# Twelve expert chunks instead of nine inside the four-head attention of a graph network, the expert biases on GpSimd, and twelve buffers for the stored parts

## The chip, the core and the metric

The kernel runs on one core of a Trainium2 chip. The metric is the device time of one execution in microseconds (us). Before the change it was 8173.12 us in the median of three runs (8167.27, 8173.12 and 8198.01).

## The reference

Four layers of a network on a graph of 6250 nodes with 256 features and 106250 edges, each added to its input: an edge adapter, six experts with a router, a graph attention of two layers with one head, and four experts whose router is a graph attention with four heads. The change lies in the last of them, of which this is the part that matters (131072 edges of its own and a loop for each of the 6250 rows):

```python
h = (x_flat @ W_gat).reshape(M, HEADS, NUM_EXPERTS)
a_src = (h * att_src).sum(-1)
a_dst = (h * att_dst).sum(-1)
e = leaky_relu(a_src[src] + a_dst[dst], negative_slope=0.2)
e_max = segment_max(e, dst)
ee = jnp.exp(e - e_max[dst])
alpha = ee / (segment_sum(ee, dst)[dst] + 1e-16)
agg = segment_sum(h[src] * alpha[:, :, None], dst).reshape(M, HEADS * NUM_EXPERTS) + b_gat
scores = layernorm(agg, ln_gamma, ln_beta).reshape(M, HEADS, NUM_EXPERTS).mean(1)
topk_s, topk_i = top_k(scores, 2)
w = softmax(topk_s, axis=-1)
for ei in range(NUM_EXPERTS):                       # 4 experts
    g = jnp.where(topk_i == ei, w, 0.0).sum(-1)
    hh = gelu(x @ W1[ei] + b1[ei])                  # 256 -> 512
    out = out + g[..., None] * (hh @ W2[ei] + b2[ei])   # 512 -> 256
```

The experts' values hh @ W2 don't depend on the router, only the gates g do. That is why the kernel can compute them before the scores are known.

## The kernel before, in words

The 6250 nodes lie in 49 blocks of 128 rows (NB), four blocks are a chunk (CB), so there are twelve full chunks and one of a single block (chunk 12, NCH). XT holds the normalized input, transposed, for all blocks. One *unit* is one chunk with one expert. A unit has eight products, each a sum over TensorE matmuls into one PSUM bank, pE: four of the first layer (128 of the 512 hidden values for 512 nodes, line 876) and four of the last layer (one block of 128 nodes by 256 values, line 881).

The four-head attention (function attention with H = 4) walks over 304 groups (NGS) of 512 edges that are sorted by their target block. Each engine has its own instruction list, written out group by group by the helper pipeline: for each iteration it calls a list of parts, each for a group that lies some groups ahead or behind. What ties the engines together are semaphores, and each engine executes its list strictly in order. In one iteration `it`

- GpSimd gathers the rows of G for a group with four indirect DMAs (line 782), up to eight groups ahead (RING);
- TensorE does lookup (pL, line 840), sums (pU, line 859), then one expert product (dense_product), then spread (pT, line 816, and pW, line 820) for the next group and turn_scores (pA, line 802) for the one behind it;
- ScalarE does dense_drain (it copies pE out, a first-layer product with its bias to hid, line 983, a last-layer product to ystage, line 987), near (ST, line 919), copies (aT, line 901), rescale (alpha, line 936), weights (p, line 967, and S, line 970), dense_gelu (the gelu over the hidden values of a unit when its fourth first-layer product has been drained, line 997), distances (Nm, line 928) and node_bits (lines 911 and 912, which turn_scores needs);
- VectorE does several_heads: the reduction mt<-pW (line 1072), pf = G x p (line 1080), and a chain of small instructions up to acc (line 1156);
- SP stores each drained last-layer block from ystage to expert_parts in DRAM (line 767).

Before the change the expert products begin in group 8 (FIRST), one in each group, and cover PRE = 9 chunks, 36 units, 288 products. First-layer products of a unit alternate with last-layer products of the unit before it (dense_step). A product may start when the one before it has been drained from pE (s_xd).

The last block (last_experts) computes the four chunks that are left, 16 units, of which the last four are of one block: hidden (pH, line 2077) and last (pO, line 2088) on TensorE, gelu and a drain to one of three buffers yr on ScalarE (lines 2107 and 2114). VectorE first computes the scores and the gates (lines 2134 to 2183), with a square root (line 2120) and an exp by ScalarE in between. Then it merges the units in the order of the list todo: the fresh ones of this block, with the 36 stored ones (yl, read back by SP through three buffers of 512 KB, line 2040) spread evenly between them. A unit gets its bias B2 (with_bias, line 2200) and is then added to X with its gate, one instruction a block (line 2210). When the last expert of a chunk has been added, SP stores the chunk's rows to the output. ScalarE's list has the first fresh unit's drain behind the square root.

Of the kernel before, what the change touches and what calls it, by code (L numbers as in the profile page):

```python
# [14 lines left out]
ALU = mybir.AluOpType  # L15
ACT = mybir.ActivationFunctionType
# [7 lines left out]
P = 128  # L24
N = 6250
D = 256
KT = D // P
NB = -(-N // P)
TAIL = N - (NB - 1) * P
CB = 4  # L30
# [19 lines left out]
RING = 8  # L50
# [6 lines left out]
HID = 512  # L57
# [4 lines left out]
PADS = P  # L62
PRE = 9
UNITS = PRE * 4
FIRST = 8
# [591 lines left out]


def attention(self, gi, H, F, table, acc, m, adst, dense=None):

# [6 lines left out]
    v = nc.vector  # L667
    one = H == 1
    NG, K = NGS[gi], KS[gi]
# [10 lines left out]
    with ctx:  # L680
# [63 lines left out]
        def _(sp):  # L744
# [12 lines left out]
            for g in range(NG):  # L757
                part, n = g // PART + 1, g - FIRST
                if g % PART == RING and 2 <= part < NG // PART:
                    sp.wait_ge(s_U, (part - 1) * PART)  # L760
                    load(part)
                if not one and 0 <= n < 8 * UNITS:
                    hidden, u, i = dense_step(n)
                    if not hidden:
                        c, x = u // NX1, u % NX1
                        sp.wait_ge(s_xd, n + 1)
                        sp.dma_start(y_dram[c * P:(c + 1) * P, (x * CB + i) * D:(x * CB + i + 1) * D], ystage[:, i, :])\
                            .then_inc(s_ys[i], 16)
# [18 lines left out]
        def _(pe):  # L787
# [74 lines left out]

            def dense_product(g, j, turn):

                n = g - FIRST
                if not 0 <= n < 8 * UNITS:
                    return
                hidden, u, i = dense_step(n)
# [16 lines left out]
            if one:  # L885
                pipeline(pe, NG, [(2, turn_scores), (1, spread), (-2, turn_weights), (-3, sums)], RING)
            else:
                pipeline(pe, NG, [(-1, lookup), (-4, sums), (0, dense_product), (1, spread), (2, turn_scores)], RING)

        @block.scalar  # L890
        def _(act):
# [79 lines left out]

            def dense_drain(g, j, turn):

                n = g - FIRST
                if not 0 <= n < 8 * UNITS:
                    return
                hidden, u, i = dense_step(n)
# [11 lines left out]
            def dense_gelu(g, j, turn):  # L989

                n = g - FIRST
                if not 0 <= n < 8 * UNITS:
                    return
                hidden, u, i = dense_step(n)
                if hidden and i == HID // P - 1:
                    act.wait_ge(s_xd, n + 1)
                    a.activation(hid[u % 2], hid[u % 2], ACT.Gelu).then_inc(s_gelu, 1)

            if one:
                pipeline(act, NG, [(0, score), (0, rescale), (2, copies), (3, node_bits), (-2, copy_weights), (0, weights)], RING)  # L1000
            else:
                pipeline(act, NG, [(0, dense_drain), (1, near), (2, copies), (0, rescale), (-1, weights), (0, dense_gelu),
                                   (1, distances), (3, node_bits)], RING)

# [985 lines left out]
def last_experts(self, XT, acc, dense):  # L1990
# [6 lines left out]
    left = [(c, e) for c in range(PRE, NCH + 1) for e in range(E)]  # L1997
    SLOTS, RY = 3, 3
    ctx, sb, ps, sem = self.scope()
    with ctx:  # L2000
# [6 lines left out]
               sb("yr2", [P, CB, D])[:, :, :]]  # L2007
        yl = sb("yl", [P, RY, CB, D])
        bg, ga, be = (sb(x, [P, NH]) for x in ("bg", "ga", "be"))
# [18 lines left out]
        def blocks(c):  # L2028
            return min(CB, NB - c * CB)

        todo, ready = [], [(c, e) for c in range(PRE) for e in range(E)]
        for n, unit in enumerate(left):
# [4 lines left out]
        def _(sp):  # L2037
            def load(n):
                c, e = ready[n]
                sp.dma_start(yl[:, n % RY, :, :].rearrange("p i d -> p (i d)"),  # L2040
                             y_dram[c * P:(c + 1) * P, e * CB * D:(e + 1) * CB * D]).then_inc(s_yl[n % RY], 16)
# [8 lines left out]
            for n, (c, e) in enumerate(todo):  # L2050
# [12 lines left out]
                if c == NCH:  # L2063
                    sp.dma_start(self.out[(NB - 1) * P:N, :], self.X[0:TAIL, NB - 1, :]).then_inc(s_out, 16)
                    outs += 1
            sp.wait_ge(s_out, 16 * outs)

        @block.tensor
# [60 lines left out]
        def _(dve):  # L2129
# [54 lines left out]

            def part(unit):
                cc, e = unit
                n = blocks(cc)
                if cc < PRE:
                    return yl[:, ready.index(unit) % RY, 0:n, :]
                return yr[left.index(unit) % SLOTS][:, 0:n, :]  # L2190

            def with_bias(n):
                cc, e = todo[n]
                if cc < PRE:
                    k_ = ready.index(todo[n])
                    dve.wait_ge(s_yl[k_ % RY], 16 * (k_ // RY + 1))
                else:
                    dve.wait_ge(s_od, left.index(todo[n]) + 1)
                t = part(todo[n])
                v.tensor_tensor(t, t, B2[:, e, :].unsqueeze(1).to_broadcast([P, blocks(cc), D]), ALU.add).then_inc(s_t, 1)  # L2200

            def add(n):
# [9 lines left out]

            with_bias(0)
            for n in range(len(todo)):
                nxt = n + 1 < len(todo)
                if nxt:
                    with_bias(n + 1)
                add(n)
# [72 lines left out]
```

## Time and profile before

| | before |
|---|---|
| median of three runs | 8173.12 us |
| profiled execution | 8179.65 us |
| span of its trace | 8177.9 us |
| four-head attention, first to last reduction | 6373.8 to 7944.6 us |
| last block, first product to end of the span | 7960.1 to 8177.9 us |
| last addition of the last block ends | 8173.2 us |
| busy over the whole span: TensorE, VectorE, ScalarE, GpSimd | 54%, 66%, 44%, 72% |

A profile is of one execution. In it PE is TensorE's matmul, PEld its weight load, DVE is VectorE, ACT ScalarE, POOL GpSimd and SP the engine that issues most transfers. Times are us from the start of the span. All other blocks of the kernel, up to 6370 us, are the same in both versions.

### The profile page before, as it was taken

The page shows a single profiled execution, that of the slowest core. Times are in us where ns is not written, and L with a number is a line of the kernel's source. Part 1 is how long each engine was busy: PE and PEld are TensorE (multiplying, and loading weights), DVE is VectorE, ACT ScalarE, POOL GpSimd, SP SyncE. Part 2 cuts the span into 40 slices and gives each one's busy share as a digit, 9 for nine tenths or more (in the row PEclk, how much of TensorE's full clock was granted, in tenths as well). Part 3 has the DMA queues.
Part 4 walks back from the last instruction along what each step waited for, and adds up shares of the span by engine and source line. Part 5 has one row for each costly group of instructions (what it writes and reads, how often), then busy time and mean ns, then how long its engine had stood idle before and what let it go on. Part 6 is the DMA issues. An engine that isn't in the chain of part 4 may idle for free. (4 is left out here: it accounts for less than half of the span.)

```text
span 8177.9 us, 116177 instructions
## 1 busy us (share of the span) xinstructions
PE 4396.1 (54%) x22490; PEld 2786.9 (34%) x22610; DVE 5392.1 (66%) x18777; ACT 3584.6 (44%) x11436; POOL 5852.7 (72%) x6709
## 2 busy tenths in 40 slices
PE   0000008915269992466666656666612677777768
PEld 0000007912135551344444434444411344444435
DVE  9999308913112221577777767777741899999987
ACT  0000003401012220277777547777721688888872
POOL 2777777777777777777777777777777777777750
PEclk9999999956589996699999979999966799999989
DMA  5111111200010000134434323444310211111113
GB/s 160 26 25 26 24 22 42 47 2 3 2 29 1 1 1 1 51 107 108 108 108 108 84 74 107 108 108 108 107 29 5 41 28 27 28 27 28 28 32 117
DMA packets 476255, 426.34 MB, mean 52 GB/s; under 512 B 269726, under 2 KB 409876, under 8 KB 475668
## 3 DMA queue, kind: packets, MB, share of 16 engines
q0 software_dynamic: 214016, 282.62, 15.0%
q1 hardware_dynamic: 224020, 120.13, 5.4%
q10 hardware_dynamic: 37632, 17.48, 0.9%
q14 instruction: 428, 3.51, 0.1%
q8 instruction: 159, 2.61, 0.1%
HBM read 341.50 MB, written 78.72 MB: 51 GB/s over the span
## 5 line engine op out<-in xcount | busy, mean ns | idle before, releaser
L438 POOL DMA_INDIRECT pay_sorted<-pay,pos x1856 | 1857.5, 1001 | 667.6 <-issue 291.9
L782 POOL DMA_INDIRECT G<-tab_gat,pay x1856 | 1788.9, 964 | 591.4 <-issue 559.0
L782 POOL DMA_INDIRECT G<-tab_rt,pay x1216 | 1154.4, 949 | 427.5 <-issue 298.0
L275 POOL DMA_INDIRECT attr_sorted<-rows,pos x832 | 841.4, 1011 | 389.2 <-issue 253.1
L856 PE MATMUL pU<-G,PM 128*128 128x257 f32 x3712 | 994.0, 391 | 2.5 <-DVE acc L1169 2.4
L802 PE MATMUL pA<-identb,G 128*20 128x128 bf16 (+1 forms) x3072 | 388.5, 226 | 943.8 <-DMA G<-tab_gat,pay 810.6
L901 ACT ACTIVATE aT<-pA 20x256 bf16<-20x256 bf16 (+1 forms) x1232 | 519.2, 421 | 527.3 <-PE pA L802 517.8
L1072 DVE TENSOR_REDUCE mt<-pW 128x4 f32<-128x2048 f32 x304 | 694.5, 2285 | 14.3 <-PE pW L820 12.9
L856 PEld LDWEIGHTS pU<-G,PM 128*128 128x128 f32 x3712 | 652.6, 196 | 59.0 <-ACT PM L953 3.0
L802 PEld LDWEIGHTS pA<-identb,G 128*20 128x20 bf16 (+1 forms) x3072 | 163.9, 92 | 1451.7 <-DMA G<-tab_gat,pay 1196.7
L323 ACT ACTIVATE rows<-lo 128x16 f32<-128x16 f32 x52 | 11.6, 229 | 1138.4 <-DMA attr_sorted<-rows,pos 1078.8
L947 ACT ACTIVATE e<-pW,adst 128x256 f32<-128x256 f32 x928 | 431.2, 465 | 172.9 <-DVE mt L1045 127.0
L1045 DVE TENSOR_REDUCE mt<-pW 128x1 f32<-128x256 f32 x928 | 390.7, 421 | 124.8 <-PE pW L812 116.9
L1673 DVE TENSOR_TENSOR t<-pO,BL 128x1024 f32<-128x1024 f32 (+1 forms) x78 | 90.7, 1163 | 573.7 <-PE pO L1620 573.6
L1657 ACT ACTIVATE H<-pH,B 128x512 f32<-128x512 f32 (+1 forms) x312 | 206.5, 662 | 593.0 <-PE pH L1609 592.1
L1169 DVE SCALAR_TENSOR_TENSOR acc<-acc,alpha,pU 128x257 f32 x928 | 442.6, 477 | 25.9 <-issue 17.4
L962 ACT ACTIVATE PT<-e,bias 128x256 f32<-128x256 f32 x928 | 456.5, 492 | 0.7 <-DVE e L1161 0.7
L1161 DVE SCALAR_TENSOR_TENSOR e<-e 128x256 f32<-128x256 f32 x928 | 397.7, 429 | 36.9 <-ACT e L947 2.9
L928 ACT ACTIVATE Nm<-iota,pay 128x128 bf16<-128x128 f32 x1216 | 383.2, 385 | 0.0
L828 PE MATMUL pP<-ident,PT 128*128 128x128 f32 x1856 | 364.3, 279 | 0.0
L336 PE MATMUL turned<-ident,gsum 128*1 128x128 f32 x24 | 5.6, 411 | 632.7 <-DVE gsum L406 632.7
L953 ACT ACTIVATE PM<-pP 128x256 f32<-128x256 f32 x928 | 332.0, 358 | 8.5 <-PE pP L828 7.8
(327 smaller groups left out, 11639.2 us busy)
## 6 DMA issues: line engine op xcount, KB each, us to landing
pay_sorted<-pay,pos POOLq DMA_INDIRECT x1856, 2.1
G<-tab_gat,pay POOLq DMA_INDIRECT x1856
G<-tab_rt,pay POOLq DMA_INDIRECT x1216, 2.4
expert_parts<-pos SPq DMA_DIRECT2D x144, 128.0 KB, 1.7
yl<-expert_parts SPq DMA_DIRECT2D x36, 512.0 KB, 3.8
attr_sorted<-zattr SPq DMA_DIRECT2D x1, 16896.0 KB, 53.4
rows<-attr_sorted ACTq DMA_DIRECT2D x256, 66.0 KB
attr_sorted<-rows,pos POOLq DMA_INDIRECT x832, 2.2
```

The lines of the kernel that those rows point to most:

```text
L275: pool.indirect_dma_start(out=self.attr_sorted, out_offset=bass.IndirectOffsetOnAxis(ap=pos0[:, t:t + 1], axis=0), in_=rows[:, j, k, :], i ...
L438: pool.indirect_dma_start(out=out, out_offset=bass.IndirectOffsetOnAxis(ap=self.pos[g][:, lo + n:lo + n + 1], axis=0), in_=self.pay[g][:, ...
L782: pool.indirect_dma_start(out=G[:, j, k, 0:R], out_offset=None, in_=table, in_offset=bass.IndirectOffsetOnAxis(ap=pay[:, g % (2 * PART), k ...
L802: ins = nc.tensor.transpose(pA[j % len(pA)][:, k * P:(k + 1) * P], parts[:, k, 0:ROWS], self.identb[:, :])
L856: ins = nc.tensor.matmul(u[:, 0:F], PM[:, j % 2, k * P:(k + 1) * P], G[:, j, k, 0:F], start=(k == 0), stop=(k == K - 1))
L901: a.activation(aT[0:ROWS, j % 2, :], pA[j % len(pA)][:, 0:K * P], ACT.Copy).then_inc(s_aT, 1)
L947: a.activation(e[:, j % 2, :], pW[j % 2][:, 0:K * P], ACT.Identity, bias=ad).then_inc(s_y, 1)
L962: a.activation(PT[:, s, :], e[:, s, :], ACT.Exp, bias=bias[:, j % 4:j % 4 + 1]).then_inc(s_PT, 1)
L1045: v.tensor_reduce(mt, pW[s][:, 0:K * P], AX.X, ALU.max).then_inc(s_max, 1)
L1072: v.tensor_reduce(mt, pW[:, :, :], AX.X, ALU.max).then_inc(s_max, 1)
L1161: v.scalar_tensor_tensor(e[:, j % 2, :], e[:, j % 2, :], SLOPE, e[:, j % 2, :], ALU.mult, ALU.max).then_inc(s_e, 1)
L1169: v.scalar_tensor_tensor(ac, ac, alpha[:, j, 0:1], pU[j % 2][:, 0:F], ALU.mult, ALU.add).then_inc(s_acc, 1)
```

## The change

PRE goes from 9 to 12, so that all twelve full chunks are computed inside the attention: 48 units, 384 products. The function quanta says which products a group takes: two in every third group from group 8 on, one in the others, 384 in 288 groups. The second product of a group is the last of TensorE's iteration, and its drain stands behind weights on ScalarE. In the last block only chunk 12, one block of 128 rows, is left to compute, four units. The stored parts, now 48, come back through twelve buffers, which lie in the columns of XT that no one reads any more. The biases are added by GpSimd, in the order of todo, and VectorE keeps the gated additions.

```diff
-PRE = 9
+PRE = 12
...
+def quanta(g):
+
+
+    at = g - FIRST
+    if at < 0:
+        return []
+    n = at + (at + 2) // 3
+    return [x for x in (n, n + 1)[:2 if at % 3 == 0 else 1] if x < 8 * UNITS]
...
             def dense_product(g, j, turn):
-
-                n = g - FIRST
-                if not 0 <= n < 8 * UNITS:
-                    return
+                for n in quanta(g)[0:1]:
+                    product(n)
+
+            def second_product(g, j, turn):
+                for n in quanta(g)[1:2]:
+                    product(n)
...
-                pipeline(pe, NG, [(-1, lookup), (-4, sums), (0, dense_product), (1, spread), (2, turn_scores)], RING)
+                pipeline(pe, NG, [(-1, lookup), (-4, sums), (0, dense_product), (1, spread), (2, turn_scores), (0, second_product)], RING)
...
-                pipeline(act, NG, [(0, dense_drain), (1, near), (2, copies), (0, rescale), (-1, weights), (0, dense_gelu),
-                                   (1, distances), (3, node_bits)], RING)
+                pipeline(act, NG, [(0, dense_drain), (1, near), (2, copies), (0, rescale), (-1, weights), (0, second_drain),
+                                   (0, dense_gelu), (1, distances), (3, node_bits)], RING)
...
-    SLOTS, RY = 3, 3
+    SLOTS, RY = 3, 12
...
-        yl = sb("yl", [P, RY, CB, D])
+        of_k = RY // KT
+
+        def yl(n):
+            return XT[:, n % RY // of_k, n % of_k * CB * D:(n % of_k + 1) * CB * D]
+
...
+        @block.gpsimd
+        def _(pool):
+            pool.wait_ge(s_w, 64)
+            for n, (c, e) in enumerate(todo):
+                if c < PRE:
+                    k_ = ready.index((c, e))
+                    pool.wait_ge(s_yl[k_ % RY], 16 * (k_ // RY + 1))
+                else:
+                    pool.wait_ge(s_od, left.index((c, e)) + 1)
+                t = part((c, e))
+                pool.tensor_tensor(t, t, B2[:, e, :].unsqueeze(1).to_broadcast([P, blocks(c), D]), ALU.add).then_inc(s_t, 1)
+
...
-            with_bias(0)
             for n in range(len(todo)):
-                nxt = n + 1 < len(todo)
-                if nxt:
-                    with_bias(n + 1)
                 add(n)
```

How the instructions lie on the engines is shown at three places; in the rows a number x4 is a count of equal instructions, and the line numbers of the changed kernel are some 10 to 40 higher. First TensorE, one iteration in the middle of the attention, before:

```order
L840 MATMUL pLU<-tabs,pay 128x24 x4
L859 MATMUL pLU<-pfs,pay 128x60 x4
L876 MATMUL pE<-XT,W 128x512 x2
L816 MATMUL pT<-aT,sel 128x512
L820 MATMUL pW<-aT,sel 128x512 x4
L802 MATMUL pA<-identb,G 28x128 x4
```

The same place in the changed kernel, an iteration of a group with two products:

```order
L850 MATMUL pLU<-tabs,pay 128x24 x4
L869 MATMUL pLU<-pfs,pay 128x60 x4
L891 MATMUL pE<-XT,W 128x512 x2
L826 MATMUL pT<-aT,sel 128x512
L830 MATMUL pW<-aT,sel 128x512 x4
L812 MATMUL pA<-identb,G 28x128 x4
L896 MATMUL pE<-W,pay 128x256 x4
```

The second product, a last-layer one, stands between turn pA and the next iteration's lookup. Next ScalarE, from the drain of a unit's fourth first-layer product over its gelu to the next drain, before:

```order
L983 ACTIVATE pay<-pE,B 128x512
L919 ACTIVATE pay<-pT 128x512
L901 ACTIVATE aT<-pA 28x512
L936 ACTIVATE alpha<-dm 128x4
L967 ACTIVATE p<-d 128x16
L970 ACTIVATE pay<-Nm 128x512
L997 ACT_TABLE_LOAD
L997 ACTIVATE pay<-pay 128x2048
L928 ACTIVATE Nm<-iota,pay 128x128 x4
L911 ACTIVATE G<-pay 128x4x8
L912 ACTIVATE G<-pay 128x4x8
L987 ACTIVATE pos<-pE 128x256
```

And the changed kernel, from the second drain of the group before it to the gelu:

```order
L1007 ACTIVATE pos<-pE 128x256
L943 ACTIVATE Nm<-iota,pay 128x128 x4
L926 ACTIVATE G<-pay 128x4x8
L927 ACTIVATE G<-pay 128x4x8
L1003 ACTIVATE pay<-pE,B 128x512
L934 ACTIVATE pay<-pT 128x512
L916 ACTIVATE aT<-pA 28x512
L951 ACTIVATE alpha<-dm 128x4
L982 ACTIVATE p<-d 128x16
L985 ACTIVATE pay<-Nm 128x512
L1015 ACT_TABLE_LOAD
L1015 ACTIVATE pay<-pay 128x2048
```

A second drain now stands ahead of the distances, the bits and all that follows them up to the gelu. Last VectorE in the last block, from the gates on, before:

```order
L2183 TENSOR_TENSOR pos<-pos 128x196
L2200 TENSOR_TENSOR pos<-pos,B_21 128x1024
L2200 TENSOR_TENSOR yl<-yl,B_21 128x1024
L2210 SCALAR_TENSOR_TENSOR X<-pos,X 128x256 x4
L2200 TENSOR_TENSOR yl<-yl,B_21 128x1024
L2210 SCALAR_TENSOR_TENSOR X<-yl,pos,X 128x256 x4
L2200 TENSOR_TENSOR pay<-pay,B_21 128x1024
```

VectorE at the same place in the changed kernel:

```order
L2223 TENSOR_TENSOR pos<-pay,m_21 128x196
L2224 TENSOR_TENSOR pos<-pos 128x196
L2234 SCALAR_TENSOR_TENSOR X<-pos,X 128x256
L2234 SCALAR_TENSOR_TENSOR X<-XT,pos,X 128x256 x48
L2234 SCALAR_TENSOR_TENSOR X<-pay,pos,X 128x256
```

And GpSimd there, which had no instruction in this block before:

```order
L690 UNCONDITIONAL_BRANCH
L2097 UNCONDITIONAL_BRANCH
L2107 TENSOR_TENSOR pos<-pos,B_21 128x256
L2107 TENSOR_TENSOR XT<-XT,B_21 128x1024 x12
L2107 TENSOR_TENSOR pay<-pay,B_21 128x256
```

The biases have moved from VectorE to GpSimd, and the first of them is that of the first fresh unit; twelve stored parts follow each fresh one.

## Rows read from the trace of the kernel before

**Rows 1.** Busy us and counts of each engine by stretch, clock, DMA share.

```profile
6900.00:7100.00 200.00, 146.24 (x874) 82.07 (x889) 187.90 (x812) 162.55 (x473) 146.72 (x155) 0.97 0.17 28
8140.00:8160.00 20.00, 1.61 (x8) 1.08 (x6) 18.44 (x36) 0.69 (x2) 0.00 (x0) 0.62 0.62 196
```

**Rows 2.** One line's instructions (ns min/median/max, first and last start), and one wait.

```profile
L1072 DVE TENSOR_REDUCE mt<-pW x304: 2283/2284/2292, 6373.8 to 7944.6; 128x4 f32<-128x2048 f32 x152
...
L997 ACT ACTIVATE pay<-pay x36: 1909/1910/1914, 6434.8 to 7884.5; 128x2048 f32<-128x2048 f32 x36
...
DVE pf L1080 <- ACT p L967: 12.2, 28, 2.0
```

**Rows 3.** Timeline (start, us, engine, line) of one undisturbed period of the attention.

```profile
7031.96 2.28 DVE L1072 TENSOR_REDUCE mt<-pW 128x4 f32<-128x2048 f32 x1
...
7032.54 1.97 PE L881 MATMUL pE<-W,pay 128*128 128x256 f32 x8
...
7035.52 0.40 PE L802 MATMUL pA<-identb,G 128*28 128x128 bf16 x4
...
7036.64 0.61 ACT L970 ACTIVATE pay<-Nm 128x512 bf16<-128x512 bf16 x1
...
7036.99 2.28 DVE L1072 TENSOR_REDUCE mt<-pW 128x4 f32<-128x2048 f32 x1
...
7037.22 0.25 PE L840 MATMUL pLU<-tabs,pay 128*128 128x24 bf16 x4 [1.31 <-DVE acc L1156]
```

**Rows 4.** Timeline from a gelu's table load to the late pf and the next turn.

```profile
7010.91 1.28 ACT L997 ACT_TABLE_LOAD   x1
...
7015.66 0.38 PE L802 MATMUL pA<-identb,G 128*28 128x128 bf16 x4 [1.40 <-ACT G L912]
...
7018.39 0.24 DVE L1080 TENSOR_TENSOR pf<-G,p 128x80 f32<-128x80 f32 x1 [0.44 <-ACT p L967]
...
7020.42 0.38 PE L802 MATMUL pA<-identb,G 128*28 128x128 bf16 x4 [1.36 <-ACT G L912]
```

**Rows 5.** Chain that ended last (start, us, what): first, middle and last piece.

```profile
7960.11 15.91 PE pH L2077 x32
...
8129.38 1.03 ACT yr L2114
...
8172.37 0.79 DVE X L2210 x2
```

**Rows 6.** Timeline of the last block: square root, gates, two units' additions.

```profile
7978.23 0.24 ACT L2120 ACTIVATE mu<-var 128x49 f32<-128x49 f32 x1 [7.05 <-DVE var L2157]
...
7993.87 0.36 DVE L2183 TENSOR_TENSOR pos<-pos 128x196 f32<-128x196 f32 x1
...
8131.58 1.67 DVE L2210 SCALAR_TENSOR_TENSOR X<-yl,pos,X 128x256 f32<-128x256 f32 x4
...
8134.30 1.67 DVE L2210 SCALAR_TENSOR_TENSOR X<-yr,pos,X 128x256 f32<-128x256 f32 x4
```

**Rows 7.** Timeline of a period with a slow product.

```profile
7000.26 2.29 DVE L1072 TENSOR_REDUCE mt<-pW 128x4 f32<-128x2048 f32 x1
...
7000.84 3.16 PE L881 MATMUL pE<-W,pay 128*128 128x256 f32 x8
...
7005.61 2.29 DVE L1072 TENSOR_REDUCE mt<-pW 128x4 f32<-128x2048 f32 x1 [0.23 <-PE pW L820]
```

**Rows 8.** GpSimd's groups by line (count, busy us, mean ns, idle before).

```profile
L254 POOL MEMSET zattr<- 128x256 f32 x1 | 0.3, 311 | 0.7 <-POOLq L126 0.7
...
L190 POOL TENSOR_SCALAR_AFFINE_SELECT ident<-ident 128x128 f32<-128x128 f32 x1 | 0.3, 292 | 0.2 <-POOL identb L187 0.2
```

**Rows 9.** Timeline of GpSimd's scatters beside VectorE in the six-expert layer.

```profile
3005.26 0.97 POOL L438 DMA_INDIRECT pay_sorted<-pay,pos  x1 [0.30 <-issue]
...
3006.19 1.67 DVE L1680 SCALAR_TENSOR_TENSOR X<-t,g,X 128x256 f32 x4
...
3006.73 1.19 POOL L438 DMA_INDIRECT pay_sorted<-pay,pos  x1 [0.28 <-POOL idle L443]
```

More of the change, by code:

```diff
@@ L757, in _ @@
             for g in range(NG):
-                part, n = g // PART + 1, g - FIRST
+                part = g // PART + 1
                 if g % PART == RING and 2 <= part < NG // PART:
@@ L761, in _ @@
                     load(part)
-                if not one and 0 <= n < 8 * UNITS:
+                for n in () if one else quanta(g):
                     hidden, u, i = dense_step(n)
@@ L863, in dense_product, with product @@
             def dense_product(g, j, turn):
-                n = g - FIRST
-                if not 0 <= n < 8 * UNITS:
-                    return
+                for n in quanta(g)[0:1]:
[3 more added lines that the diff above has]
+                    product(n)
+            def product(n):
                 hidden, u, i = dense_step(n)
@@ L972, in dense_drain, with second_drain, drain @@
             def dense_drain(g, j, turn):
-                n = g - FIRST
-                if not 0 <= n < 8 * UNITS:
-                    return
+                for n in quanta(g)[0:1]:
+                    drain(n)
+            def second_drain(g, j, turn):
+                for n in quanta(g)[1:2]:
+                    drain(n)
+            def drain(n):
                 hidden, u, i = dense_step(n)
@@ L989, in dense_gelu @@
             def dense_gelu(g, j, turn):
[L991 to L997, printed above, removed]
+                for n in quanta(g):
+                    hidden, u, i = dense_step(n)
+                    if hidden and i == HID // P - 1:
+                        act.wait_ge(s_xd, n + 1)
+                        a.activation(hid[u % 2], hid[u % 2], ACT.Gelu).then_inc(s_gelu, 1)
             if one:
@@ L2029, in blocks, with part @@
             return min(CB, NB - c * CB)
+        def part(unit):
+            cc, e = unit
+            n = blocks(cc)
+            if cc < PRE:
+                return yl(ready.index(unit)).rearrange("p (i d) -> p i d", d=D)[:, 0:n, :]
+            return yr[left.index(unit) % SLOTS][:, 0:n, :]
         todo, ready = [], [(c, e) for c in range(PRE) for e in range(E)]
@@ L2039, in load @@
                 c, e = ready[n]
-                sp.dma_start(yl[:, n % RY, :, :].rearrange("p i d -> p (i d)"),
+                sp.dma_start(yl(n),
                              y_dram[c * P:(c + 1) * P, e * CB * D:(e + 1) * CB * D]).then_inc(s_yl[n % RY], 16)
@@ L2183, in _ @@
             c(v.tensor_tensor(g[:, :, :], a[:, :, :], b[:, :, :], ALU.add))
[L2185 to L2200, printed above, removed]
             def add(n):
```

## The prediction, made before the changed kernel was run

> **What bounds the kernel now.** I first asked where the kernel can change at all. All edits lie in the last two blocks, the four-head attention and the block of the last experts, so I read those two alone: first busy time by stretch, then single periods, then the chain that ended last. In the middle of the attention VectorE is busy for 187.9 of 200 us, ScalarE for 162.6, TensorE for 146 and GpSimd for 147 [rows 1]. One period of the loop is one group, and the longest instruction in it, VectorE's reduction mt<-pW, marks its start. 304 reductions start between 6373.8 and 7944.6 [rows 2], a mean of 5.18 us; an undisturbed period lasts 5.03 (7031.96 to 7036.99), with a product in it (pE<-W) [rows 3]: one product hides. VectorE sets the pace, and about 303 x 0.15 = 45 us of the block are lost elsewhere.
>
> The reader should look at ScalarE after a gelu. Table load and gelu take 1.28 and 1.91 us [rows 2, 4]; the bits that turn pA needs stand behind them, so TensorE waits 1.40 us for ScalarE, and behind that the weights p come late: VectorE's pf waits 0.44 us for them [rows 4]. Over the block pf waits 12.2 us for p, 28 times for 36 gelus [rows 2].
>
> In the last block the chain runs along TensorE's products from 7960.11 to the last drain at 8129.38, then along VectorE to 8173.16 [rows 5]: TensorE bounds it, with a tail on VectorE of 2.72 us a unit (8131.58 to 8134.30), of which 1.67 us are the four additions and the other 1.05 the bias, L2200 [rows 6].
>
> **Part 1, products in the attention.** 96 more products (12 units of 8) are fitted into the same 288 groups: every third group has a second product, which TensorE runs behind turn pA, as its last work of the period. Laid on the undisturbed period [rows 3]: turn pA ends 3.96 us after the reduction's start, and the next lookup starts at 5.26, so 1.30 us are free; the product takes 1.97. It runs 0.67 us into the next period, where the lookup has room. But its drain is queued on ScalarE behind S (which ends at 5.29) and waits for the product: 3.96 + 1.97 + 0.38 = 6.3, with the semaphores 1.33 us into the next period. The next product shares pE and waits for this drain: it starts at 1.35 and not at 0.58, so everything that ScalarE does behind its own drain is 0.78 us later in that period. Without a gelu the third group recovers this, and I cost that at nothing: the cover is the slack of ScalarE and TensorE against VectorE's 5.03; without it each second product costs what a slow product costs below.
>
> With a gelu it isn't recovered. A unit's last first-layer drain always falls in the group right behind a double one (it is product 8u+2, and the groups take products 4k and 4k+1, then 4k+2, then 4k+3 in turn), so each gelu starts 0.78 us later than now, and pf waits 0.44 + 0.78 = 1.22 us. There are 48 gelus then: 58.6 us against 12.2, +46. The delayed period is itself a double one. Its pf comes at about 2.2 + 1.22 = 3.4 us, the bits some 2.0 us behind it as now (7018.39 to 7020.42) [rows 4], and its first drain, 0.7, behind these: 6.2. Only then can its second product start; it ends 1.9 us into the next period (which begins at 6.25), its drain at 2.3, and that period's own product and spread (1.97 and 1.2, partly overlapped) at about 5.4: 0.37 us over 5.03. 48 x 0.37 = +18. Together **+64 us**.
>
> Bounds: if the later start is absorbed, only 12 more gelus at 12.2/36 = 0.34 us remain, +4. At the other end, where a product took 3.16 us and not 1.97 the period grew to 5.35 (7000.26 to 7005.61) [rows 7]; if each of the 96 costs these 0.32 us besides, +95. GpSimd's gathers and SP's stores stay behind the same groups; a store has six groups before its buffer is needed again, and I put it at nothing.
>
> **Part 2, the last block.** Twelve of its full units leave TensorE; four units of one 128-row block stay. So TensorE's 169 us go, and the next late thing is the merging: 48 stored parts and 4 small ones, a bias each (now on GpSimd) and 196 additions on VectorE.
>
> When GpSimd can start: its first operation belongs to the first fresh unit, whose drain is queued on ScalarE behind the square root of the router's variances, which ends at 7978.47 [rows 6]. Then a table load of 1.28, four small gelus and the drain, about 1.8 together: 7981.5, or 21.5 us into the block. All 48 stored parts wait behind that operation. VectorE has the gates at 7994.2 [rows 6].
>
> Price of a bias on GpSimd (128x1024, two inputs): no row shows one. Below, a write of 256 elements takes 0.311 us, and one input and one output of 128 take 0.292 us [rows 8]. Taking 0.1 as fixed, the second is 1.5 ns an element, or 1.6 us for 1024, the low end; three streams at the write's 0.9 ns an element make 2.9 us, the high end. VectorE's 1.05 us is below both. I take the middle, 2.3 us: 48 x 2.3 + 4 x 0.65 = 113 us. The Trainium skill's GPSIMD Engine Reference (section Performance versus the Vector engine) gives 4497 ns for an addition of 2048 elements; by that an estimate is 2.25 us each and the sum 2 us less.
>
> Additions: 196 x 1.67/4 = 82 us. The question that decides the block is whether they run beside GpSimd's biases or in turn with them. The rows have a hint: a GpSimd scatter takes 0.97 us, and 1.19 where VectorE runs the same kind of addition, both inputs in SBUF (L1680, four in 1.67 us) [rows 9]. So the two get in each other's way there by 0.22 us. If each addition costs GpSimd only 0.22, that is 43 us; if they exclude each other, 82. The scatter has one column of offsets as its operand there, a bias reads 2048 elements a partition in SBUF, which speaks for the larger price. The Trainium skill, SBUF — State Buffer (section SBUF: two separate sides), says more than the row: an exclusive lock, held for the whole instruction, between a GpSimd instruction that reads SBUF and a VectorE one with two SBUF inputs. By it the 82 us count in full; by the row the sum would be 39 us less.
>
> In turn: 21.5 + 113 + 43 to 82, and 4 for the dozen gate operations caught in it: 181 to 220 against 213 now (7960.1 to 8173.2), so -32 to +7; the store behind it stays. VectorE's adds wait 2.3 us behind a bias but the biases also stop at the twelfth buffer, so the sum is what counts. I take **-8**, on the side of the larger price. Side by side: 21.5 + 113 + 1.7 = 136, so **-77**.
>
> Loads: twelve of them are issued ahead of the merging. In turn each unit has 3.5 us for 512 KB and a quarter of an equal store, 187 GB/s; in 8140 to 8160 the queues moved 196 GB/s at a share of 0.62 [rows 1]. Side by side it is 285 GB/s, under 196/0.62 = 316. Hidden in both.
>
> **Sum.** +64 - 8 = +56 us. The profiled execution took 8179.65 us, 6.5 above the median of the three runs, 8173.12; against the median I forecast 8173 + 56 = **8229 us**, 0.7% slower. A measurement of this kernel tells about 0.5% (41 us) from no change.
>
> **Rivals.**
> 1. *Side by side, dear attention.* GpSimd paces the merging and VectorE hides under it: +64 - 77 = -13, 8160 us, no measurable change. For it: the 0.22 us of the scatter are small beside its 0.97; against it, that they are there at all.
> 2. *In turn, cheap attention.* The second products hide as the first ones do: +4 - 8 = -4, 8169 us. For it: the 5.03 us with a product inside; against it the queue order on ScalarE.
> 3. *Faster.* The merging at GpSimd's own pace: -77. It decides from the point where the attention costs less than 36 us; with +4 it is -73, 8100 us. For it: the last block's 169 us of TensorE do go, and nothing that shows in its rows takes their place but 113 us of GpSimd.
> That the change doesn't do what it says I leave out: the order of instructions shows the products, the biases and the loads where they are meant to be.
>
> **How the numbers follow.** I hold turns at 0.62 against side by side, and a dear attention at 0.65. Forecast 0.41, rival 1 0.21, rival 2 0.19, rival 3 0.14, and 0.05 for a time above all (+95 and +7: 8275). The forecast's own range is 8205 to 8275. For 8 in 10 the range must take in rivals 1 and 2 and most of 3: **8095 to 8275**. Faster by over 0.5%: rival 3 and a part of rival 1, 0.18. Slower: most of the forecast and the dearest case, 0.41. Within: 0.41.
>
> **What would show it.** In the changed profile: reductions still 304, their first and last start some 64 us further apart, and waits of pf for p near 60 us where they were 12. The last block: a bias on GpSimd of 2 to 2.5 us when VectorE rests; start to start 3.3 to 4 us a unit if in turn, about 2.3 if side by side, with additions of 0.48 us unlengthened. The block should be within 30 us of 213 in the first case and near 136 in the second. I am wrong if pf's waits stay near 12 us, if a bias takes under 1.6, or if loads of expert_parts are what VectorE or GpSimd wait for.

## The result, and the profile after

| | before | after |
|---|---|---|
| median, us | 8172.36 | 8332.02 (8285.51 to 8349.58) |
| ratio | | 1.0173, interval 1.0148 to 1.0199 |
| profiled execution (span), us | 8179.65 (8177.9) | 8328.67 (8326.9) |
| first reduction of the four-head attention | 6373.8 | 6401.8 |
| attention, first to last reduction | 1570.8 | 1690.3 |
| last reduction to the end | 233.3 | 234.8 |

The medians are of four runs each. Two executions in the record, one of the kernel before (14606 us) and one of the version "order of three" below (10298 us), ran at a granted clock of 0.38 and 0.67 and are left out of every range and ratio here. The change made the kernel 1.7% slower; the forecast was 8229 us and its range ended at 8275. The span grew by 149 us: 28.0 ahead of the first reduction, in blocks that the change leaves alone, 119.5 in the attention (forecast 64), 1.5 in the last block (forecast -8).

Busy time of each engine by stretch in the kernel after, as in [rows 1]; the number behind the five engines is TensorE's granted clock as a share of 2.4 GHz:

```profile
6401.80:8092.10 1690.30, 1400.20 (x7288) 747.98 (x7435) 1504.07 (x6341) 1377.31 (x3858) 1146.73 (x1205) 0.90 0.16 28
...
6900.00:7100.00 200.00, 167.84 (x862) 89.33 (x879) 175.74 (x740) 162.81 (x451) 135.12 (x143) 0.90 0.17 29
```

VectorE, which paced the loop with 187.9 of 200 us, is busy for 175.7 now: it waits more. The clock went from 0.97 to 0.90. The waits of the attention, by line (us, times, longest):

```profile
PE pA L812 <- ACT G L927: 135.2, 54, 2.9
...
DVE pf L1098 <- ACT p L982: 67.3, 48, 1.7
...
PE pE L891 <- ACT pos L1007: 25.1, 94, 1.2
```

The second of them answers to the last of [rows 2]: 67.3 us in 48 waits where there were 12.2 in 28. That is the late p behind a gelu, forecast at 58.6. It accounts for 55 of the 119.5 us. The rest shows when two places of the same kind are laid side by side. (A double group is one with two products; it is behind a gelu where it lies two groups after that of the gelu, and without one otherwise.) First a double group without a gelu and the group behind it, at full clock, from the timeline (start, us):

```profile
7245.64 2.28 DVE L1090 TENSOR_REDUCE mt<-pW 128x4 f32<-128x2048 f32 x1
...
7245.87 0.25 PE L850 MATMUL pLU<-tabs,pay 128*128 128x24 bf16 x4 [1.29 <-DVE acc L1174]
...
7246.23 1.96 PE L891 MATMUL pE<-XT,W 128*128 128x512 f32 x4
...
7249.20 0.40 PE L812 MATMUL pA<-identb,G 128*28 128x128 bf16 x4
7249.52 1.99 PE L896 MATMUL pE<-W,pay 128*128 128x256 f32 x8
7250.66 2.29 DVE L1090 TENSOR_REDUCE mt<-pW 128x4 f32<-128x2048 f32 x1
7251.55 0.38 ACT L1007 ACTIVATE pos<-pE 128x256 f32<-128x256 f32 x1 [0.62 <-PE pE L896]
...
7251.99 1.98 PE L891 MATMUL pE<-XT,W 128*128 128x512 f32 x4 [0.26 <-ACT pos L1007]
...
7255.68 2.28 DVE L1090 TENSOR_REDUCE mt<-pW 128x4 f32<-128x2048 f32 x1
```

This is the forecast within 0.1 us: the second product starts 3.88 us into its period (3.96), its drain ends 1.27 into the next (1.33), the next product starts at 1.33 (1.35), and both periods last 5.02 us. Now the same kind of place a little earlier:

```profile
7179.46 2.29 DVE L1090 TENSOR_REDUCE mt<-pW 128x4 f32<-128x2048 f32 x1
...
7179.69 0.25 PE L850 MATMUL pLU<-tabs,pay 128*128 128x24 bf16 x4 [1.90 <-DVE acc L1174]
...
7180.19 3.28 PE L891 MATMUL pE<-XT,W 128*128 128x512 f32 x4
...
7184.85 0.40 PE L812 MATMUL pA<-identb,G 128*28 128x128 bf16 x4
...
7184.96 2.29 DVE L1090 TENSOR_REDUCE mt<-pW 128x4 f32<-128x2048 f32 x1 [0.40 <-DMA rows<-in_edge_attr_dram]
7185.18 1.99 PE L896 MATMUL pE<-W,pay 128*128 128x256 f32 x8
7187.21 0.38 ACT L1007 ACTIVATE pos<-pE 128x256 f32<-128x256 f32 x1 [0.62 <-PE pE L896]
...
7187.65 1.98 PE L891 MATMUL pE<-XT,W 128*128 128x512 f32 x4 [0.26 <-ACT pos L1007]
...
7190.75 2.29 DVE L1090 TENSOR_REDUCE mt<-pW 128x4 f32<-128x2048 f32 x1 [0.27 <-PE pW L830]
```

The first product takes 3.28 us, so turn pA comes 5.39 us into the period and not 3.56, the second product starts only in the next period, and that period's own product 2.69 into it. The two periods take 5.50 and 5.79 us, 1.25 over two of 5.02. (The releaser that the second reduction names, a load at the kernel's start, is of no use: the last recorded product of spread pW ended 0.25 us before.) The clock tells why, by stretch, TensorE alone (busy, count, clock):

```profile
7179.46:7184.96 5.50, 4.99 (x18) 0.69 0.13 14
7245.64:7250.66 5.02, 4.65 (x25) 1.00 0.11 14
```

The 0.69 is a mean of the clock's two levels, 1.2 GHz for a part of the period and 2.4 GHz for the rest; just before, TensorE had waited 1.90 us for VectorE's acc, at the other place 1.29.

In the timeline of the whole attention 79 products are slow, that is, take over 2.3 us; before there were 25 of them. The trace has as many stretches at the lower clock in the attention, 79 and 25. Of 48 double groups without a gelu 38 have a slow first product, mean periods of it and of the next group 5.42 and 5.79 us with it and 5.10 and 5.15 without; of 48 behind a gelu 41 have one, 6.75 and 5.48 us with it and 6.03 and 5.50 without.

In the last block, the timeline from GpSimd's first bias to the first addition:

```profile
8128.98 1.23 POOL L2107 TENSOR_TENSOR pos<-pos,B 128x256 f32<-128x256 f32 x1 [50.86 <-ACT pos L2155]
...
8130.18 28.52 POOL L2107 TENSOR_TENSOR XT<-XT,B 128x1024 f32<-128x1024 f32 x12
...
8137.42 2.38 DVE L2212 TENSOR_TENSOR pos<-pos,r 128x196 f32<-128x196 f32 x1
8139.84 0.36 DVE L2213 TENSOR_REDUCE k<-pos 128x49 f32<-128x196 f32 x1
...
8160.42 0.48 DVE L2234 SCALAR_TENSOR_TENSOR X<-pos,X 128x256 f32<-128x256 f32 x1
...
8202.60 2.34 POOL L2107 TENSOR_TENSOR XT<-XT,B 128x1024 f32<-128x1024 f32 x1 [1.45 <-DMA XT<-expert_parts]
...
8202.72 2.50 DVE L2234 SCALAR_TENSOR_TENSOR X<-pay,pos,X 128x256 f32<-128x256 f32 x1
```

The block starts at 8107.6 us; the first bias comes 21.4 later (forecast 21.5) and a full one takes 2.34 (forecast 2.3). Beside a bias an addition takes 2.50 us and not 0.48: it is held until the bias ends. The gates of the router are held in the same way: one with two inputs takes 2.38 where before the same took 0.36, while the reduction between takes 0.36. So the first addition comes 52.8 us into the block; before it came 36.4 in (from 7960.1 to 7996.5). The two rows of before:

```profile
7984.90 0.36 DVE L2171 TENSOR_TENSOR pos<-pos,r 128x196 f32<-128x196 f32 x1
...
7996.54 1.67 DVE L2210 SCALAR_TENSOR_TENSOR X<-pos,X 128x256 f32<-128x256 f32 x4
```

By line in the kernel after, with shapes (busy, mean ns, idle before):

```profile
L2234 DVE SCALAR_TENSOR_TENSOR X<-XT,pos,X 128x256 f32<-128x256 f32 x192 | 148.2, 831 | 5.0
L2107 POOL TENSOR_TENSOR XT<-XT,B 128x1024 f32<-128x1024 f32 x48 | 115.0, 2406 | 55.1 <-DMA XT<-expert_parts 55.1
```

The additions' mean went from 0.48 to 0.83 us: 36 of 196 were held and took 2.4 to 2.7 us. GpSimd waited 55.1 us for loads, but a load is issued only when VectorE has emptied a buffer, so that wait may follow from VectorE's; the first run below tests it.

### The profile page after: what moved, and what is told of

Its sections match the earlier page's. It is cut to its first block and busy times, and to the rows that moved or that the text cites. A ratio compares the mean times of both kernels' runs of the same rounds, so it can differ in the third digit from the quotient of the medians.

```text
span 8326.9 us, 116351 instructions
## 1 busy us (share of the span) xinstructions
PE 4479.4 (54%) x22462; PEld 2797.8 (34%) x22610; DVE 5466.9 (66%) x18725; ACT 3647.5 (44%) x11508; POOL 5999.4 (72%) x6761
## 5 line engine op out<-in xcount | busy, mean ns | idle before, releaser
L792 POOL DMA_INDIRECT G<-tab_gat,pay x1856 | 1807.9, 974 | 591.6 <-issue 561.4
L891 PE MATMUL pE<-XT,W 128*128 128x512 f32 x768 | 484.0, 764 | 25.7 <-ACT pos L1007 25.1
L896 PE MATMUL pE<-W,pay 128*128 128x256 f32 x1536 | 382.2, 392 | 0.9 <-ACT pos L1007 0.3
```

Source lines behind the costliest of these rows:

```text
L792: pool.indirect_dma_start(out=G[:, j, k, 0:R], out_offset=None, in_=table, in_offset=bass.IndirectOffsetOnAxis(ap=pay[:, g % (2 * PART), k ...
L891: ins = nc.tensor.matmul(pE[:, :], W1[:, x, k, i * P:(i + 1) * P], XT[:, k, c * CB * P:(c + 1) * CB * P], start=(k == 0), stop=(k == KT - 1))
```

## The experiments

All are compared by the stretch in which they differ, in the profiled execution of each; times are us, slow products are those over 2.3 us. Biases on VectorE, no gelu, filler and filler 2 were run once each. The same attention took 1655.4 to 1690.3 us in three executions, and such differences have to be kept in mind.

| kernel | first reduction | attention | slow products | wait for p | last reduction to end |
|---|---|---|---|---|---|
| before | 6373.8 | 1570.8 | 25 | 12.2 | 233.3 |
| after | 6401.8 | 1690.3 | 79 | 67.3 | 234.8 |
| after, again | 6400.3 | 1655.4 | 52 | 59.0 | 234.7 |
| biases on VectorE | 6394.9 | 1677.4 | 69 | 65.2 | 185.3 |
| no gelu | 6428.0 | 1565.9 | 16 | none | 234.3 |
| filler | 6429.8 | 1658.3 | 32 | 46.8 | 234.3 |
| filler 2 | 6430.3 | 1612.4 | 1 | 49.3 | 234.7 |
| mended | 6380.6 | 1610.9 | 1 | 47.2 | 185.5 |
| order of three | 6375.9 | 1568.3 | 25 | 12.6 | 209.4 |
| larger table | 6368.3 | 1571.1 | 27 | 13.3 | 234.0 |
| ten chunks | 6367.4 | 1575.7 | 25 | 13.3 | 189.4 |

**Biases back on VectorE.** The changed kernel with this edit (dots stand for lines left out, here and below):

```
-        @block.gpsimd
-        def _(pool):
...
+            with_bias(0)
             for n in range(len(todo)):
+                if n + 1 < len(todo):
+                    with_bias(n + 1)
                 add(n)
```

> The changed kernel with the biases of the last block back on VectorE; the 12 buffers and the attention stay. Theory (GpSimd's biases and VectorE's additions run in turn, and the turn costs 2.34 us a part on GpSimd where VectorE itself needs 1.22): the last block, from the last reduction of the attention to the end, goes from 219 us to 34 + 48 x 2.72 + 4 x 0.9 + 4 = 172 us (165 to 180), additions are all near 0.48 us and none over 1, and the kernel takes some 46 us less than the changed one. Rival (the loads set the pace; in the changed kernel GpSimd waited 55 us for loads in front of its biases): the block stays over 205 us and VectorE waits for loads of expert_parts.

The last block by line with shapes, and its stretch from the last reduction on:

```profile
L2232 DVE SCALAR_TENSOR_TENSOR X<-XT,pos,X 128x256 f32<-128x256 f32 x192 | 82.5, 531 | 0.1
L2222 DVE TENSOR_TENSOR XT<-XT,B 128x1024 f32<-128x1024 f32 x48 | 60.9, 1269 | 0.0
...
8072.30:8257.60 185.30, 21.86 (x124) 19.12 (x124) 165.63 (x332) 16.23 (x37) 0.00 (x0) 0.56 0.52 174
```

The block is 49.5 us shorter (46 expected), no addition is over 0.6 us, VectorE waits for no stored part. The 172 us expected for the block, and the 219 before, count from the block's first product, not from the last reduction as the text says; counted so it went from 219.3 to 169.8 us, and from the last reduction from 234.8 to 185.3. With one more task on VectorE the block is faster: GpSimd's biases did not take work off it but held it for 2.34 us each where its own take 1.27. The loads are not what set the pace.

**No gelu.** The changed kernel without the gelus of the attention:

```
-                        a.activation(hid[u % 2], hid[u % 2], ACT.Gelu).then_inc(s_gelu, 1)
+                        a.activation(hid[u % 2][:, i, 0:1], hid[u % 2][:, i, 0:1], ACT.Copy).then_inc(s_gelu, 1)
```

> The changed kernel with each of the 48 gelus of the attention cut to a copy of one column, so the gelu itself is left out of the hidden layer there. Three causes are held for the attention's 119.5 us more: late p behind a gelu (67 us of waits for p where there were 12), and double groups whose first product ran at the fallen clock (3.2 to 3.6 us, 79 of 96). Theory A (the clock falls by itself in the new pattern, whatever the gelu does): waits for p fall under 15 us, but some 40 to 96 slow products stay, the double groups still cost 0.4 + 0.7 us, and the attention takes 1690 - 90 = 1600 us (1580 to 1620). Theory B (the clock falls because TensorE idles 2 to 3 us behind a gelu): under 25 slow products, and the attention takes 1530 to 1560 us, below the 1571 of the kernel before.

```profile
6428.00:7993.90 1565.90, 1319.38 (x7435) 724.18 (x7435) 1476.87 (x6342) 1182.55 (x3762) 1147.28 (x1205) 0.96 0.17 31
```

The attention's stretch is 1565.9 us, 6 over the band of theory B and 14 under that of A; the clock is back at 0.96, the slow products are 16. So the fall hangs on the gelu, also in the double groups without one, some 20 us behind the last gelu (38 slow products to 10 there). This doesn't yet tell the clock from the late p, as both went.

**Work without use on TensorE.** The first filler adds four products in each group that has only one:

```
+            def filler(g, j, turn):
+                if len(quanta(g)) == 1:
+                    pe.wait_ge(s_ST, g + 2)
+                    for _ in range(4):
+                        nc.tensor.matmul(pT[:, :], sel[:, 0, :], sel[:, 0:4, :].rearrange("p h c -> p (h c)"), start=True, stop=True)
...
```

> The changed kernel with four more products of 128x512 bf16 on TensorE in each group that has one product, behind the turn pA, into pT, where the next spread overwrites them: 4 x 0.21 us of work without use, in time that TensorE has free there. Theory (the double groups cost because the clock falls and their first product then takes 3.2 to 3.6 us): if the clock then stays up, slow products drop from 79 to under 25, the double group without a gelu and the group behind it go from 5.42 and 5.79 to 5.02 and 5.06 us, those behind a gelu from 6.75 to 5.9, and the attention goes from 1690 to 1610 us (1595 to 1630). Rival (the second product and its late drain cost this at any clock): the pitches stay within 0.1 us though slow products are gone, and the attention stays over 1675. If the slow products stay, the run tells nothing but that this much work doesn't hold the clock.

The slow products in double groups without a gelu went from 38 to 1, and these groups and the next from 5.35 and 5.66 us, over all of them, to 5.10 and 5.13: the theory held there. Behind the gelus it didn't: 31 of 48 stayed slow, and that period grew to 7.1 us where they did, probably since the filler also stands behind the late turn pA there. The attention fell by 32 us and not by 80, no more than executions of the same instructions differ. The second filler leaves those places and fills TensorE's wait itself:

```
+            def gelu_filler(g, j, turn):
+                if not one and gelu_in(g - 3):
+                    pe.wait_ge(s_aT, g)
+                    for _ in range(18):
+                        nc.tensor.transpose(pA[0][:, 0:P], sel[:, 0, 0:ROWS], self.identb[:, :])
...
```

> The changed kernel with work without use on TensorE at other places than in the run called filler: 18 turns of 128x28 into pA ahead of turn pA in the group in which the gelu runs, where TensorE waited 2 to 3 us for ScalarE's bits, and four 128x512 products into pT only in the two groups of six that have one product and neither follow a gelu nor a delayed double group. The first filler cured the double groups without a gelu (slow products 38 to 1, 5.42 to 5.09 us) but left 31 slow products in the double groups behind a gelu, whose period grew to 7.1 where the product was slow. Theory (these too are long because the clock fell while TensorE waited): slow products behind a gelu fall from 31 to under 15, that period goes from 6.72 to about 6.0 and the next from 5.64 to 5.3, the attention takes 1615 us (1600 to 1635) where filler took 1658. Rival (the late p alone sets that period): it stays at 6.6 or more at either clock, the attention stays over 1645.

The attention's stretch, and the wait for p:

```profile
6430.30:8042.70 1612.40, 1433.67 (x8687) 795.77 (x8687) 1479.43 (x6342) 1372.11 (x3858) 1147.07 (x1205) 0.98 0.17 30
...
DVE pf L1113 <- ACT p L997: 49.3, 48, 1.4
```

With 17% more matrix instructions (8687 where the same attention had 7435) the attention is 77.9 us shorter (1615 expected, 1612.4 measured): the clock is 0.98, one product is slow. Against the second execution of the changed kernel below it is 43.0 us shorter. The period behind a gelu is 6.21 us, the next 5.26. What is left over the kernel before, 41.6 us, is as much as the late p, 49.3 against 12.2, and 4.5 more; what the work without use itself costs no run tells.

**Both mends, and the changed kernel once more.** The first is filler 2 with the biases on VectorE.

> The changed kernel with both mends at once: the work without use on TensorE as in filler2, and the biases on VectorE as in bias_dve. Theory (the losses are separate and add up: the fallen clock 78 us in the attention, the turn-taking of GpSimd and VectorE 49 us in the last block): attention 1612 us (1600 to 1625), last block from the last reduction 185 us (180 to 190), from the first reduction to the end 1797 where the changed kernel took 1925 and the kernel before 1804; the ratio to the kernel before 0.995 to 1.000, or up to 1.007 where the gathers ahead of the attention are slow as in the other kernels with twelve chunks. Rival (one loss covers another, so that one mend gives back what the other gained): over 1830 from the first reduction to the end.

> The changed kernel once more, as it is, for the 28 us ahead of the attention. Theory (the slow gathers come and go from one execution to the next): its times spread by 25 to 65 us, some at 8285 to 8295, where the first reduction of the attention starts near 6374, and others at 8310 to 8350; the ratio lies at 1.015 to 1.018. Rival (they belong to this program): all its times lie above 8305, and the first reduction starts at 6394 or later.

Mended: 1796.4 us from the first reduction to the end (1797 expected), ratio 0.999 (0.9972 to 1.0008). Its attention took 1610.9 us, so two executions with the work without use lie at 1611 and 1612 and three without it at 1655 to 1690. The losses are separate and add up; with both taken away the changed kernel is as fast as the one before, not faster.

The changed kernel again: ratio 1.015 (1.0117 to 1.0182), times from 8280.52 to 8351.97 us. Its profiled execution took 8292.15 us, and of this the theory was wrong: the first reduction started at 6400.3, late as ever, and the time was saved in the attention, with 52 slow products in place of 79. This is a test that no edit made: three executions have the same instructions in the attention. From 79 slow products to 52 it lost 34.9 us, or 1.29 each; by that line the 69 of the kernel with biases on VectorE give 1677.4, and 1677.4 was measured. By the line it would take 1588 us with none, 24 less than filler 2 with one; whether this is the price of the work without use, no run tells.

**The 28 us ahead of the attention.**

```
-                y = nc.dram_tensor("expert_parts", (PRE * P, NX1 * CB * D), F32).ap()
+                y = nc.dram_tensor("expert_parts", (12 * P, NX1 * CB * D), F32).ap()
```

> The kernel before with the table of stored parts in device memory made for twelve chunks; nine are still used, no instruction differs but in addresses. In the four kernels with twelve chunks the first reduction of the four-head attention started at 6395, 6402, 6428 and 6430, in the two with nine at 6374 and 6376, and gathers of tab_gat took 974 to 989 ns against 964, in blocks that the change doesn't touch. Theory (the placement in memory that the larger table causes): it starts 20 us or more late here too, 6394 to 6430. Rival (it belongs to something else in the changed program, its longer code): 6374 to 6380, gathers at 964 ns, and the time is that of the kernel before.

Ratio 0.9997 (0.9984 to 1.001), and the first and last reduction start early:

```profile
L1072 DVE TENSOR_REDUCE mt<-pW x304: 2283/2285/2293, 6368.3 to 7939.4; 128x4 f32<-128x2048 f32 x152
```

The larger table is not the cause. The gathers of the one-head layers are, in part. By line, before:

```profile
L782 POOL DMA_INDIRECT G<-tab_gat,pay x1856 | 1788.9, 964 | 591.4 <-issue 559.0 <-DMA pay<-pay_sorted 26.6 <-PE pU L856 5.8
```

and after:

```profile
L792 POOL DMA_INDIRECT G<-tab_gat,pay x1856 | 1807.9, 974 | 591.6 <-issue 561.4 <-DMA pay<-pay_sorted 26.5 <-PE pU L866 3.7
```

1807.9 against 1788.9 us is 19 of the 28. In profiled executions with twelve chunks they took 968 to 989, in the others 961 to 964; but the kernel before itself ranges from 8167 to 8210 us, and the mended kernel started its attention at 6380.6. Whether the longer program does this or only meets it more often stays open.

**Two other versions.** The kernel before with three stored parts behind each of the first twelve new units:

```
-            todo += ready[n * len(ready) // len(left):(n + 1) * len(ready) // len(left)]
+            todo += ready[3 * n:3 * n + 3]
```

> The kernel before with one line changed: three stored parts follow each of the first twelve new units in the last block, none the last four small ones, where 2 or 3 followed each of all sixteen. VectorE idled in the first half and had a tail of 44 us. Expected: the attention is unchanged within 5 us, the last block goes from 218 to 189 us (182 to 198), the kernel 29 us faster (0.3 to 0.4 per cent). Rival (VectorE's additions hold back the fresh units, whose three buffers then stop TensorE): the block stays over 210 us. This kernel stores nine chunks, as the kernel before, and its profile tells whether the 28 us that the changed kernel lost ahead of the attention belong to the larger table of stored parts: then the first reduction of the four-head attention starts within 8 us of 6374 here and near 6402 in the three kernels with twelve chunks.

From the last reduction it takes 209.4 us where it took 233.3, so the block goes from 218 to 194: within the band, a little dearer than 189. Ratio 0.9978 (0.9963 to 0.9993).

And ten chunks, with one double group in most units, away from the gelu:

```
+        two = doubles and n % 8 == 6
+        doubles -= 1 if two else 0
+        table.append([n, n + 1] if two else [n])
...
+QUANTA = quanta_table(32)
...
```

> A version drawn from the runs so far: ten chunks in the attention, where 32 of the 40 units have one double group each, two groups behind which no gelu is due; biases on VectorE as in the kernel before; ten buffers; five stored parts behind each of the first eight new units. Theory (a double group costs little where no gelu and no fallen clock meet it; the last block is bound by VectorE's 2.72 us a part): the attention takes 1578 us (1570 to 1592) where the kernel before took 1571, the last block, from the last reduction to the end, 185 us (180 to 192) as in bias_dve where it was 233, slow products at most 40. The kernel takes 40 us less than before, ratio 0.995 (0.993 to 0.997), if the blocks ahead of the attention stay as they were; with 20 to 56 us more there, as in the kernels with twelve chunks, 0.998 to 1.002. Rival (a second product costs about 1 us wherever it stands): the attention takes over 1600 and the ratio is over 0.998 in either case.

Attention and last block by stretch:

```profile
6367.40:7943.10 1575.70, 1220.57 (x7051) 665.03 (x7051) 1477.23 (x6342) 1304.73 (x3770) 1142.18 (x1205) 0.95 0.16 28
...
7943.10:8132.50 189.40, 130.92 (x508) 89.63 (x508) 165.63 (x332) 45.37 (x77) 0.00 (x0) 0.83 0.45 148
```

Expected were 1578 and 185; 32 more products cost 5 us in the attention and bring no more slow products (25). Ratio 0.9966 (0.995 to 0.9983): this version beats both kernels, by 0.3% the one before. How much of that the ten chunks bring is not shown: the order of the stored parts alone took 23.9 of the 43.9 us off the last block, and its ratio's interval overlaps this one.

## Why the prediction was wrong, step by step

- *What bounds it; a product hides; the second product's place in the period*: right within 0.1 us at full clock.
- *Late p behind a gelu, 58.6 us*: right in kind and near in size. It was 67.3 and 59.0 in the changed kernel, 49.3 with the clock held.
- *The period behind it, 0.37 us each*: 0.23 with the clock held (5.26 against 5.03), so too dear. The whole full-clock part, forecast at +64, was +41.6 in filler 2.
- ***"Without a gelu the third group recovers this, and I cost that at nothing"***: this step failed. It holds at full clock, but it took the clock of [rows 1], 0.97, for granted, and so did the steps behind a gelu. In the changed pattern the clock fell 79 times where it fell 25, and holding it took off 77.9 of the 119.5 us. Laid side by side, 38 slow products without a gelu cost 0.96 us each (5.42 and 5.79 against 5.10 and 5.15), 41 behind one 0.70 (6.75 and 5.48 against 6.03 and 5.50): 36 and 29 us of the 77.9.
- ***"without it each second product costs what a slow product costs below"***, 0.32 us: the bound was too low for the same reason. [Rows 7] show a slow product with nothing queued behind it. In a double group its delay pushes the second product into the next period and the product after it as well; by the three executions it is 1.29 us each. 96 x 0.32 = 31 was the end of the range; 79 x 1.29 is 102.
- *Start of GpSimd 21.5, bias 2.3 us, in turn and not side by side*: right (21.4 and 2.34). The bias is partly luck: the 0.1 us taken as fixed stand in no row, and the write gives 0.82 ns an element with them taken off and not 0.9, which makes the high end 2.6 us and the middle 2.1. The rule of the Trainium skill that the forecast leaned on for the larger price, in SBUF — State Buffer (section SBUF: two separate sides), agrees with the trace: an addition of 0.48 us took 2.50 beside a bias.
- *"4 for the dozen gate operations caught in it"*: mis-sized. Twelve biases ran back to back (28.52 us) over the gates, and the first addition came 16.4 us later into its block than before. The additions counted in full, 82 us and not the 66.5 that -8 leaves for them. Sum: 52.8 + 36 x 2.34 + 82 = 219; the last addition ended 214.4 us into the block. So +1.5 in place of -8.
- *Loads hidden*: right in effect; with biases on VectorE they ran at 237 to 252 GB/s and nobody waited.
- *The blocks ahead*: not in the sum, and 28.0 us; 19 of them are the dearer gathers, whose cause stays open.

From +56 to +149: 77.9 for the clock, -22.4 for the rest of the attention, 9.5 in the last block, 28.0 ahead of it.

## What to carry to other kernels

An engine's slack at its present clock is not a spare resource if filling it can change the clock: here the added products came with 52 to 79 slow ones in place of 25. Where TensorE waits on another engine each few groups, ask what one slow product delays behind it, not what it costs alone. Before moving elementwise work to GpSimd, look whether VectorE works with two SBUF inputs at the same time; here the two then took turns, and their times added up. Move out of a block only what its bound holds up: ten chunks cost the attention 5 us, twelve 85 to 120.

## What the runs showed of the hardware

- The granted clock of TensorE depends on the execution: the same attention had 52, 69 and 79 slow products. Work without use, at the right places, brought it from 0.90 to 0.98 and made the attention 78 us shorter, or 43 against the execution with 52. The Trainium skill, TensorE: Matmul & The Clock Gate (section HAM oscillation — how this bites in real kernels), tells of a loop that pays for a fallen clock in each turn because of a wait in it, there for a transfer; here the wait is for ScalarE's bits (135.2 us, 54 times), 41 of the 48 places behind a gelu pay, and so far the trace agrees. In front of the slow products without a gelu TensorE had waited too, but for VectorE's acc and for less: 1.43 to 2.02 us, with a median of 1.67, and 1.29 to 1.96, with a median of 1.50, in front of those that stayed fast (the attention's first left out). The ranges overlap, so the length of this wait alone doesn't tell when the clock falls; what else decides stays open.
- Beside GpSimd's biases VectorE's reductions keep their time (0.36 us), its two-input operations don't (0.36 to 2.38), and a one-input operation didn't either: L2207 in the changed kernel, 2.20 us where its like took 0.17 with the biases on VectorE. Two others of its kind went from 0.26 to 1.42 and from 0.19 to 1.96. First the row of the changed kernel, then that with the biases on VectorE:

```profile
8132.69 2.20 DVE L2207 TENSOR_SCALAR r<-iota 128x4 f32<-128x4 f32 x1
```

```profile
8111.67 0.17 DVE L2195 TENSOR_SCALAR r<-iota 128x4 f32<-128x4 f32 x1
```
